# A graph attention layer in f32 on one core: the last of six layer parts in products of 192 columns instead of 384

## What is computed

```python
def gat_conv(x, src, dst, W, a_src, a_dst, b):          # H = 4 heads, C = 192
    h = (x @ W).reshape(N, H, C)
    as_n = (h * a_src).sum(-1)
    ad_n = (h * a_dst).sum(-1)
    e = leaky_relu(as_n[src] + ad_n[dst], 0.2)
    m = segment_max(e, dst);  p = exp(e - m[dst]);  s = segment_sum(p, dst)
    alpha = p / (s[dst] + 1e-16)
    return segment_sum(alpha[:, :, None] * h[src], dst).reshape(N, H * C) + b

x1 = relu(x @ W_ah + b_ah)
xs = [relu(gat_conv(x1, src, dst, W, a_s, a_d, b)) for the three layers]
out = layernorm(x + relu(concatenate(xs, axis=1) @ W_out + b_out))
```

## Time and profile before

| | us |
|---|---|
| median of three runs | 988.29 |
| lowest, highest of them | 986.38, 988.45 |
| profiled execution, its own time | 986.58 |
| its span, first to last instruction | 984.9 |

### The profile page before, as it was taken

One profiled execution on the slowest core, in us unless ns is written; L12 is line 12 of the kernel. 1 busy time (PEld: TensorE's weight loads), 2 busy tenths in 40 slices (PEclk: granted clock), 3 DMA queues, 4 the chain that ended last, 5 costly groups with the idle time before them and its releaser, 6 DMA issues. The chain is left out here.

```text
span 984.9 us, 14408 instructions
## 1 busy us (share of the span) xinstructions
PE 957.5 (97%) x5560; PEld 885.8 (90%) x5560; DVE 760.3 (77%) x1064; ACT 365.2 (37%) x524; POOL 22.0 (2%) x34
## 2 busy tenths in 40 slices
PE   6999999999999999999999999999999999999997
PEld 3677765999999999999999999999999869999996
DVE  5999998799999659997997998988878173234223
ACT  1444523121222144555556365465465461001000
POOL 1000000000000000001000000010010000000000
PEclk9999999999999999999999999999999999999999
DMA  5123172255344481316218136138632173323211
GB/s 171 37 65 135 35 252 76 93 163 163 117 135 137 117 234 53 92 40 132 90 42 166 52 97 111 53 90 273 207 92 69 48 189 114 121 79 110 79 32 32
DMA packets 54361, 108.10 MB, mean 110 GB/s; under 512 B 10684, under 2 KB 37917, under 8 KB 53158
## 3 DMA queue, kind: packets, MB, share of 16 engines
q1 hardware_dynamic: 36740, 66.34, 22.4%
q0 software_dynamic: 4048, 18.60, 8.4%
q10 hardware_dynamic: 13522, 22.47, 7.2%
HBM read 80.31 MB, written 27.08 MB: 109 GB/s over the span
## 5 line engine op out<-in xcount | busy, mean ns | idle before, releaser
L1250 PE MATMUL ps<-R_W 125*125 125x193 f32 x2400 | 397.8, 327 | 5.0 <-ACT R_XIN L680 3.8
L1250 PEld LDWEIGHTS ps<-R_W 125*125 125x125 f32 x2400 | 391.3, 188 | 8.6 <-ACT R_XIN L680 7.5
L665 ACT ACTIVATE R_W<-R_EXP,s 125x1250 f32<-125x1250 f32 x120 | 161.2, 1344 | 162.9 <-PE ps L1250 94.5
L946 DVE SCALAR_TENSOR_TENSOR R_W<-R_W,R_CNT 125x1250 f32<-125x1250 f32 x120 | 174.6, 1455 | 3.9 <-DVE R_EXP L935 2.0
L905 DVE CUSTOM_DVE_ANT_0 R_ROWS<-R_MASK,R_ROWS 125x1250 bf16<-125x1250 bf16 x100 | 138.6, 1460 | 3.5 <-ACTq L618 3.5
L1170 PE MATMUL ps<-Wl_hi,x_hi 128*125 128x384 f32 x360 | 122.1, 339 | 0.0
L1170 PE MATMUL ps<-Wl_hi,x_lo 128*125 128x384 f32 x360 | 121.7, 338 | 0.0
L1170 PE MATMUL ps<-Wl_lo,x_hi 128*125 128x384 f32 x360 | 121.5, 338 | 0.0
L1309 PE MATMUL ps<-Wo_hi,xs_hi 128*125 128x384 f32 (+2 forms) x324 | 109.5, 338 | 0.3 <-PE ps L1299 0.3
L1309 PE MATMUL ps<-Wo_lo,xs_hi 128*125 128x384 f32 (+2 forms) x324 | 109.3, 337 | 0.0
L1309 PE MATMUL ps<-Wo_hi,xs_lo 128*125 128x384 f32 (+2 forms) x324 | 109.3, 337 | 0.0
(11 more groups left out here) (144 smaller groups left out, 850.9 us busy)
## 6 DMA issues: line engine op xcount, KB each, us to landing
xs_dram<-R_XIN POOLq DMA_DIRECT2D x18, 625.0 KB, 10.8
h_dram<-R_HOUT ACTq DMA_DIRECT2D x30, 336.0 KB
R_W<-h_dram SPq DMA_DIRECT2D x12, 840.0 KB
R_ROWS<-as_dram SPq DMA_DIRECT2D x12, 625.0 KB, 5.5
R_EXP<-u_dram SPq DMA_DIRECT2D x6, 1250.0 KB, 6.4
R_X<-u_dram SPq DMA_DIRECT2D x6, 1250.0 KB, 5.8
R_ROWS<-in_W_all SPq DMA_DIRECT2D x18, 384.0 KB, 3.3
Wo_sb<-in_W_out POOLq DMA_DIRECT2D x1, 6912.0 KB, 27.9
```

What stands on the lines that cost most here:

```text
L665: nc.scalar.activation(prob[r % PSLOTS], expo[:, r % XSLOTS], ACT.Exp, bias=s02[:, r % NT, ds(2 * p + r // NT, 1)]).then_inc(S["exp_done"], 1)
L946: nc.vector.scalar_tensor_tensor(out=prob[r % PSLOTS], in0=prob[r % PSLOTS], scalar=HUGE, in1=cntT[:, r % NT], op0=ALU.min, op1=ALU.mult). ...
L1250: ins = mm(ps[0:PT, o:o + HW], prob[r % PSLOTS][:, t * PT:(t + 1) * PT], hB[:, q, j], start=(j == 0 and t % 2 == 0), stop=(j == NT - 1), s ...
```

## The change

In the last part (n = `PARTS - 1`) each product of 384 columns is made as two, of columns 0 to 191 and 192 to 383, with the same stationary tile, into the two halves of the same place in PSUM. Of the 18 pairs of a tile the very first product has the start flag, which clears the bank's marks for both halves, and the very last one the stop flag. `C` is 192. The five parts before stay as they are.

```diff
@@ -1167,8 +1167,11 @@
                         pe.wait_ge(S["x1_lo"], k + 1)
                         pe.wait_ge(S["w_lo"], 1)
                     for i, (xx, ww) in enumerate(((x1_hi, Wl_hi), (x1_hi, Wl_lo), (x1_lo, Wl_hi))):
-                        ins = mm(place, xx[:, k, t * PT:(t + 1) * PT], ww[n][:, k],
-                                 start=(k == 0 and i == 0), stop=(k == blocks[-1] and i == 2), skip_group_check=True)
+                        cuts = (0, C, HALF) if n == PARTS - 1 else (0, HALF)
+                        for a, z in zip(cuts, cuts[1:]):
+                            ins = mm(place[:, a:z], xx[:, k, t * PT:(t + 1) * PT], ww[n][:, k, a:z],
+                                     start=(k == 0 and i == 0 and a == 0), stop=(k == blocks[-1] and i == 2 and z == HALF),
+                                     skip_group_check=True)
                 return ins
```

## The result

Three runs of the changed kernel gave 993.79, 994.25 and 996.04 us, a median of 994.25. The ratio to the kernel before is 1.0071, with a 95% interval of 1.0044 to 1.0098: slower by 4.3 to 9.7 us. The forecast of 995.3 is 1.05 us off and lies in the interval.

The account below looks back on a forecast made before the run. The prediction took TensorE's instruction stream to bound the kernel. 180 pairs at 0.044 us more each gave 7.9 us, with nothing for the surroundings; 987.4 + 7.9 = 995.3 us, stated range 987.0 to 1015.5.

Parts of the forecast that it names:

- The bound: Whole kernel: TensorE's instruction stream sets the length, so a microsecond added in the last layer part should reach the end.
- The sum: Last part: each pair takes 0.220 us against 0.176 for one product, 0.044 more, times 180: 7.9 us.
- The price, 0.110: Last part: each 192-column product takes 0.110 us, the load of its stationary tile, longer than its columns' 0.0902.
- the restarts: Where TensorE's stream starts afresh, the first two weight loads start 0.11, 0.10 and 0.11 us apart, showing the bare load.
- The bounds of 4.3 and 11.1: Last part's added us: 4.3 if a load takes 0.100 or second loads are skipped; 11.1 at the 256-column step.
- The line of the columns: TensorE's steps at 512, 384 and 256 columns: 0.447 ns a column, giving 0.0902 us for 192.
- What lies beside it: ScalarE's copies, weighted tiles and loads around the last part and the handover to attention: nothing becomes late or shorter, cost nothing.
- Column-limited products: Rival, last part: loads overlap better and only columns count, 0.8 us more, 987.4 us; chance 0.13.
- The two cases of a lost fast route: Rivals, last part: 192-column products fall to one plain record's pace, 27.0 us, chance 0.10, or a whole plain product's, 85.7, 0.15.
- the stated range: Total time, from 987.0 (column-limited, lower run level) to 1015.5 us (one plain record's pace, upper level).
- The faster case: Rival, attention: a lead of VectorE and ScalarE shrinks TensorE's 3.8 us of waits, down to 983.6 us; chance 0.04.
- The base of 987.4: Starting time for the forecast: the middle of the kernel's two run levels, near 986.5 and near 988.4 us.

Follow-up runs that it names:

- all-parts run: All six layer parts, not just the last, made in products of 192 columns, against the kernel before: 1032.92 us against 986.89, ratio 1.0468.
- run without shared tiles: Last part's 192-column products reordered so no neighbours share a stationary tile, first five parts reordered too, against the kernel before: 994.06 us against 987.63, ratio 1.0066.

## Why the prediction was right

*The bound.* TensorE's stream is the program's length. The all-parts run shows it most strongly, and attention to end takes 622.7 us before and after. One reading was loose: the prediction puts TensorE's waits at a few microseconds in the whole run, but its row holds only those of attention. The kernel before has about 20 us of them, and the two largest stand ahead of the layer parts:

```profile
PE ps L1114 <- DMA R_W<-in_xT: 7.3, 1, 7.3
PE ps L1079 <- DVE R_EXP L818: 6.3, 9, 1.6
```

The last part also has one, of 1.1 us in front of its transposes, and it is 1.1 us with the change too. None of them touches the sum.

*The sum.* 7.9 us was forecast and the stretch gives 7.6. The price, 0.110, came from the ten small transposes, 0.111 us a load; the products measured 0.109. That row alone could not tell a load from a fixed cost of any small transpose: ten others in the last part, with 24 stationary and 125 moving columns, take (1.23 - 0.27) / 9 = 0.107 us each, though their stationary tile has a fifth of the columns.

```profile
338.00 1.23 PE L1224 MATMUL ps<-ident,u_place 125*24 125x125 f32 x10
```

They fit the pace of the plain 4-byte records of attention, 0.163 / 193 = 0.845 ns a moving column, an estimate of 0.106 us for 125. What supported the price before the result were the restarts; what proved it were the runs with 64 stationary columns. The bounds of 4.3 and 11.1 were wider than needed. The lower one stood for a skipped second load, which the run without shared tiles rules out.

*The line of the columns*, taken from 512, 384 and 256 and followed down to 192 and 128, holds below 256 once the load is short: 0.089 measured for 0.090, and 0.061 for 0.062.

*What lies beside it.* Costed at nothing, and the handover into attention kept its 0.77 us. The first weighted tile, which was done 1.1 us ahead of the last copy, is now 2.6 us ahead of it (368.71 against 371.34), and nothing uses the margin.

*The rivals.* Column-limited products are what the case of 64 stationary columns shows, at 0.3 to 0.9 us; with 125 they are not. The two cases of a lost fast route, 27.0 and 85.7 us, had 0.25 of the chance and were wrong: the rounded 4-byte type keeps its pace down to 128 columns, 0.061 us. At 64 columns, the narrowest tried, the step of 0.058 is above the 0.033 of the line, and the pace can't be read from it. No row of before could exclude these cases, though the upper end of the stated range was paid for one of them. Its lower end, 987.0, does not follow from what is said of it: 986.6 + 0.8 is 987.4. The faster case fell because TensorE's waits in attention stayed at 3.8 us.

*The time.* 995.3 against 994.25. The base of 987.4 was chosen between two places of the runs, near 986.5 and near 988.4. The prediction was right to see two: the 37 runs counted with the result fall into 985.38 to 987.40 and 987.63 to 988.85, by their granted clock. The forecast in the middle could be off by about 1 us whatever the price was, and it was off by 1.05, so the total does not test the 7.9; the stretches do. Against the median before, the forecast is a rise of 7.0 us, and the medians rose by 6.0.

The load's length also bears out the Trainium skill's page "TensorE: Matmul & The Clock Gate", section "LDWEIGHTS (loading the stationary operand)": its rate, one over 1.2 a column, is the 0.83 ns measured between 64 and 125 columns. The runs give 0.005 us beside it, by the two points, which is what 0.104 was short of 0.109. The f16 transposes of line 1098 differ from that rule: it would give 0.104 us for their 125 stationary columns, and they step at 0.058.

## What to carry to other kernels

The step of a matmul in a stream is the longer of its moving columns' time and the load of its stationary columns; for this 4-byte type at the full granted clock, 0.447 ns a moving column plus 0.004 us against 0.83 ns a stationary column plus 0.005. These are the figures of one kernel on one core. With 125 stationary columns a product narrower than about (0.109 - 0.004) / 0.000447 = 235 columns pays for columns that it doesn't have. That crossing is an estimate from the two lines, with 256 and 192 columns measured on either side of it. Sharing a stationary tile between neighbours did not change this. Before a product is cut, look for rows of small repeated products in the same trace: they can carry the price of the bare load. Take only rows with the same number of stationary columns, few moving columns and operands of the same size: with 125 moving columns the plain 4-byte transposes take 0.107 us for their columns, and the f16 ones have a faster load.

## What the runs showed of the hardware that was not expected

Two neighbouring products with the same stationary tile cost no less than two with different ones: 0.109 us a product either way. And a product can be as short as 0.058 us from start to start, 64 stationary by 64 moving columns, with one load for each. In f16, 125 stationary columns are loaded for every product and the step is still only 0.058 us, about half of the 4-byte load.

The start of the layer parts differs by up to 2.8 us between executions. The dip of the granted clock accounts for about 1.6 of that, 1.85 - 0.22 in the pair compared here; the rest, and why the clock falls in some executions, stays open.
